# Closing passages of a four-layer graph network: relation products taken head by head on four row tiles, and relation rows copied first on ScalarE

## What is computed

```python
k = _typed_linear(x, Wk, bk, node_type).reshape(n, H, DH)
q = _typed_linear(x, Wq, bq, node_type).reshape(n, H, DH)
v = _typed_linear(x, Wv, bv, node_type).reshape(n, H, DH)
kt = jnp.einsum('nhd,rhde->rnhe', k, a_rel)
vt = jnp.einsum('nhd,rhde->rnhe', v, m_rel)
...
att = (q[dst] * k_e).sum(-1) * mu[edge_type] / np.sqrt(DH)
```

## Time and profile before

| | |
|---|---|
| median of 3 runs | 10143.94 us (10141.95 to 10145.79) |
| the profiled execution | 10142.34 us, its span 10140.3 us |
| PE busy | 2087.1 us (21%) |
| PEld busy | 1860.1 us (18%) |
| DVE busy | 5894.1 us (58%) |
| ACT busy | 3016.3 us (30%) |
| POOL busy | 6842.0 us (67%) |

### The profile page before, as it was taken

How to read it: one execution, slowest core, us unless ns; L and a number is a source line. 1 busy time by engine, 2 the same in 40 slices (tenths; PEclk the granted TensorE clock), 3 DMA queues, 4 the chain that set the end, 5 groups by cost and what they waited for, 6 DMA issues and landing times. The chain is left out here.

```text
span 10140.3 us, 57816 instructions
## 1 busy us (share of the span) xinstructions
PE 2087.1 (21%) x14986; PEld 1860.1 (18%) x14986; DVE 5894.1 (58%) x9620; ACT 3016.3 (30%) x3211; POOL 6842.0 (67%) x7186
## 2 busy tenths in 40 slices
PE   4555465551000000004500008100023000110002
PEld 3555465550000000003400006100012000110002
DVE  8777565553545555556588876688875322432225
ACT  6333233331223332232255442354531000110002
POOL 2777677777777777774377753677743777667773
PEclk9999955555555555556855559555555555555556
DMA  4511111112333333334466654566641333223331
GB/s 99 201 28 28 31 36 34 33 29 59 98 99 114 113 112 106 104 113 137 149 215 209 215 177 152 184 210 213 216 139 59 106 106 103 91 90 103 107 107 58
DMA packets 489971, 1161.75 MB, mean 115 GB/s; under 512 B 183257, under 2 KB 278828, under 8 KB 431532
## 3 DMA queue, kind: packets, MB, share of 16 engines
q0 software_dynamic: 255936, 474.70, 17.6%
q1 hardware_dynamic: 203756, 628.83, 16.5%
q10 hardware_dynamic: 29952, 54.54, 2.1%
HBM read 669.62 MB, written 487.92 MB: 114 GB/s over the span
## 5 line engine op out<-in xcount | busy, mean ns | idle before, releaser
L832 POOL DMA_INDIRECT slots<-REC,plc_idx x1664 | 1597.7, 960 | 554.7 <-issue 505.9
L1238 POOL DMA_INDIRECT l_swp_G<-table,KVI x1664 | 1573.3, 946 | 529.1 <-issue 506.3
L940 POOL DMA_INDIRECT l_G<-table,OTHI x1664 | 1583.3, 952 | 513.3 <-issue 506.2
L1490 POOL DMA_INDIRECT l2s_G<-table,OTHI x832 | 785.1, 944 | 428.6 <-issue 253.3
L1490 POOL DMA_INDIRECT l3s_G<-table,OTHI x832 | 786.4, 945 | 301.6 <-issue 253.2
L703 PEld LDWEIGHTS plc_pr<-plc_seen,plc_otf 128*128 128x128 f32 x3328 | 842.5, 323 | 21.3 <-issue 11.9
L703 PE MATMUL plc_pr<-plc_seen,plc_otf 128*128 128x49 f32 x3328 | 844.0, 408 | 11.1 <-DVE plc_seen L618 11.0
L1073 DVE TENSOR_TENSOR l_LB<-l_RE,l_G 128x64 f32<-128x64 f32 x104 | 29.4, 283 | 1026.5 <-DMA l_G<-table,OTHI 1026.3
L1340 DVE SCALAR_TENSOR_TENSOR l_swp_QS<-l_swp_QS,KEEP,l_swp_QX 128x128 f32<-128x128 f32 x1664 | 589.4, 354 | 36.9 <-DMA l_swp_QX<-queries 9.5
L1099 DVE TENSOR_TENSOR_SCAN l_X<-l_AW,l_X 128x2244 f32<-128x2244 f32 x104 | 502.5, 4832 | 3.6
L1399 DVE TENSOR_TENSOR_SCAN l_swp_X<-l_swp_AW,l_swp_X 128x2244 f32<-128x2244 f32 x104 | 501.5, 4822 | 0.1
(11 more groups left out here) (495 smaller groups left out, 9906.7 us busy)
## 6 DMA issues: line engine op xcount, KB each, us to landing
sums<-l_ROW SPq DMA_DIRECT2D x104, 1088.0 KB, 4.3
sums<-l_swp_ROW SPq DMA_DIRECT2D x104, 1088.0 KB
l_swp_QX<-queries SPq DMA_DIRECT2D x104, 1024.0 KB, 7.8
queries<-plc_zrow SPq DMA_DIRECT2D x33, 1664.0 KB
sums<-l3s_ROW SPq DMA_DIRECT2D x52, 1032.0 KB, 4.4
plc_low<-low_rows ACTq DMA_DIRECT2D x208, 256.0 KB, 3.3
sums<-l2s_ROW SPq DMA_DIRECT2D x52, 1024.0 KB, 4.4
table<-t_row SPq DMA_DIRECT2D x98, 512.0 KB, 2.6
```

The lines of the kernel that those rows point to most:

```text
L832: pool.indirect_dma_start(out=slots, out_offset=bass.IndirectOffsetOnAxis(ap=idx[:, c % IB, j:j + 1], axis=0), in_=g.REC[:, c * CH + j, :] ...
L940: pool.indirect_dma_start(out=G[:, c % GR, j, :], out_offset=None, in_=table, in_offset=bass.IndirectOffsetOnAxis(ap=g.OTHI[:, side(c), x: ...
L1238: pool.indirect_dma_start(out=G[:, c % GR, j, :], out_offset=None, in_=table, in_offset=bass.IndirectOffsetOnAxis(ap=index[:, c * CK + j:c ...
L1490: pool.indirect_dma_start(out=G[:, c % GR, j, :], out_offset=None, in_=table, in_offset=bass.IndirectOffsetOnAxis(ap=g.OTHI[:, k, c * CK + ...
```

## The change

The relation products are taken head by head: 8 matmuls a block (keys and values x 4 heads), each with 32 rows of `kv` and 32 rows of a dense `bd` as operands and 128 columns (4 relations x 32). Head `h` starts at partition 32h, and writes PSUM bank `h`: keys in columns 0 to 127, values in columns 128 to 255. All four banks belong to one block, so `relate(n)` now waits until block n-1 is copied, where it waited for block n-2. The zeros of `bd` go, and with them their memset and the wait for it; `mu` is laid out a word for each partition and relation, by four small loads in place of one. Both halves of a row are copied by ScalarE (`pack_rows`), as its first work in a step; VectorE copies neither.

```diff
-            bd = s.sb("bd", [P, 2, R, D])
-            mu = s.sb("mu", [P, R * H])
+            bd = s.sb("bd", [P, 2, R, HD])
+            mu = s.sb("mu", [P, R])
...
-                sp.dma_start(mu[:, :], a.mu[tables].rearrange("(o r) h -> o (r h)", o=1).to_broadcast([P, R * H])).then_inc(rel_ok, 16)
-                sp.wait_ge(cleared, 1)
+                with nc.allow_non_contiguous_dma(reason="a word for each head and relation, once"):
+                    for h in range(H):
+                        sp.dma_start(mu[h * HD:(h + 1) * HD, :],
+                                     a.mu[tables][:, h:h + 1].rearrange("r o -> o r").to_broadcast([HD, R])).then_inc(rel_ok, 16)
...
-                    sp.wait_ge(packed_k, n + 1)
-                    sp.wait_ge(packed_v, n + 1)
+                    sp.wait_ge(packed, n + 1)
...
-            if not gcn:
-                if closes_l0:
-                    v.memset(g.X[:, NB - 1, :], 0.0)
-                v.memset(bd[:, :, :, :], 0.0)
+            if closes_l0:
+                v.memset(g.X[:, NB - 1, :], 0.0)
...
-            def pack_keys(n):
-                b = n % 2
-                v.wait_ge(related, n + 1)
-                if n >= 2:
-                    v.wait_ge(stored[b], 16 * (n // 2))
-                v.tensor_copy(row[:, b, :, 0:D], pk[:, 2 * b, :].rearrange("p (r w) -> p r w", r=R)).then_inc(packed_k, 1)
...
                 if n >= 2:
-                    act.wait_ge(related, n - 1)
+                    act.wait_ge(related, 2 * H * (n - 1))
...
-            def pack_values(n):
+            def pack_rows(n):
                 b = n % 2
-                act.wait_ge(related, n + 1)
+                act.wait_ge(related, 2 * H * (n + 1))
                 if n >= 2:
                     act.wait_ge(stored[b], 16 * (n // 2))
-                act.activation(row[:, b, :, D:2 * D], pk[:, 2 * b + 1, :].rearrange("p (r w) -> p r w", r=R),
-                               ACT.Copy).then_inc(packed_v, 1)
+                for m in (0, 1):
+                    o = act.activation(row[:, b, :, m * D:(m + 1) * D].rearrange("p r (h e) -> p r h e", h=H),
+                                       pk[:, :, m * P:(m + 1) * P].rearrange("p h (r e) -> p r h e", r=R), ACT.Copy)
+                o.then_inc(packed, 1)
...
                 if not gcn:
+                    if 0 <= s_ - 2 < NB:
+                        pack_rows(s_ - 2)
                     if 0 <= s_ < NB:
                         keep_kvq(s_)
-                    if 0 <= s_ - 2 < NB:
-                        pack_values(s_ - 2)
...
                 pe.wait_ge(kv_kept, n + 1)
-                if n >= 2:
-                    pe.wait_ge(packed_k, n - 1)
-                    pe.wait_ge(packed_v, n - 1)
-                pe.matmul(pk[:, 2 * b, :], kv[:, b, 0, :], bd[:, 0, :, :].rearrange("p r d -> p (r d)"), start=True, stop=True)
-                pe.matmul(pk[:, 2 * b + 1, :], kv[:, b, 1, :], bd[:, 1, :, :].rearrange("p r d -> p (r d)"),
-                          start=True, stop=True).then_inc(related, 1)
+                if n >= 1:
+                    pe.wait_ge(packed, n)
+                for m in (0, 1):
+                    for h in range(H):
+                        own = slice(h * HD, (h + 1) * HD)
+                        o = pe.matmul(pk[:, h, m * P:(m + 1) * P], kv[own, b, m, :],
+                                      bd[own, m, :, :].rearrange("p r e -> p (r e)"), start=True, stop=True)
+                        o.then_inc(related, 1)
```

More of the change, by code:

```diff
@@ L1651, in turn_layer @@
             pk = s.ps("pk", [P, 4, 512])
-            turned_h, masked_h, made_kvq, kv_kept, q_kept, related, packed_k, packed_v = (s.sem(x) for x in (
-                "turned_h", "masked_h", "made_kvq", "kv_kept", "q_kept", "related", "packed_k", "packed_v"))
+            turned_h, masked_h, made_kvq, kv_kept, q_kept, related, packed = (s.sem(x) for x in (
+                "turned_h", "masked_h", "made_kvq", "kv_kept", "q_kept", "related", "packed"))
             put = [s.sem(f"put{r}") for r in range(4)]
@@ L1736, in _ @@
                     sp.dma_start(w3[:, m, :, :], Wm[tables].rearrange("t i o -> i t o")).then_inc(rel_ok, 16)
-                sp.dma_start(mu[:, :], a.mu[tables].rearrange("(o r) h -> o (r h)", o=1).to_broadcast([P, R * H])).then_inc(rel_ok, 16)
-                sp.wait_ge(cleared, 1)
+                with nc.allow_non_contiguous_dma(reason="a word for each head and relation, once"):
+                    for h in range(H):
+                        sp.dma_start(mu[h * HD:(h + 1) * HD, :],
+                                     a.mu[tables][:, h:h + 1].rearrange("r o -> o r").to_broadcast([HD, R])).then_inc(rel_ok, 16)
                 for m, rel in enumerate((a.a_rel, a.m_rel)):
                     for h in range(H):
-                        sp.dma_start(bd[h * HD:(h + 1) * HD, m, :, h * HD:(h + 1) * HD],
+                        sp.dma_start(bd[h * HD:(h + 1) * HD, m, :, :],
                                      rel[tables, :, h].rearrange("r d e -> d r e")).then_inc(rel_ok, 16)
@@ L1948, in _ @@
             if not gcn:
-                v.wait_ge(rel_ok, 16 * 12)
+                v.wait_ge(rel_ok, 16 * 15)
                 link(v.tensor_scalar(mu[:, :], mu[:, :], float(HD) ** -0.5, None, ALU.mult))
-                keys = bd[:, 0, :, :].rearrange("p r (h e) -> p (r h) e", h=H)
-                v.tensor_tensor(keys, keys, cols3(mu[:, :]).to_broadcast([P, R * H, HD]), ALU.mult).then_inc(scaled, 1)
+                v.tensor_tensor(bd[:, 0, :, :], bd[:, 0, :, :], cols3(mu[:, :]).to_broadcast([P, R, HD]), ALU.mult).then_inc(scaled, 1)
             for s_ in range(-3, NB + LAG):
@@ L1960, in _ @@
                         mask_h(s_ + 1)
-                    if 0 <= s_ - 2 < NB:
-                        pack_keys(s_ - 2)
                 else:
@@ L2134, in _ @@
                     if s_ == 0:
-                        pe.wait_ge(rel_ok, 16 * 12)
+                        pe.wait_ge(rel_ok, 16 * 15)
                         pe.wait_ge(scaled, 1)
```

## The result

The changed kernel takes 10061.84 us (median of 4 runs, 10059.76 to 10066.9); the kernel before, on the same chip, 10142.94 (4 runs, 10140.65 to 10145.79). The ratio is 0.992, with a 95% interval of 0.9907 to 0.9933: 81 us faster.

A forecast was written before the change was run, and what follows sets the result against it. TensorE was taken to bound both passages, its relation products setting the time for blocks 4 to 46. Savings of 22.5 us in t0 and 21.9 in t1, together 44.4 off 10142.3, gave 10098; range 10068 to 10178.

The forecast's parts named there:

- the sixteen records: A step's relation products on TensorE, two records for each of eight matmuls: 0.90 us taken, in place of 1.77.
- the three bounds: Possible cost of the relation products' records in a step: 1.79 us in a line, 0.90, or 0.45 with four heads side by side.
- the case in which neighbours in the stream wait: TensorE's relation products: a head's two records queue and the next head comes behind both, 0.90 us; chance 0.46.
- full overlap: Rival for TensorE's relation products: four heads side by side, 0.45 us, step 4.05, 81 us gained, 10061; chance 0.12.
- Changing the tiling: TensorE, twice in a step: idling when the array's tiling mode changes, 0.18 us each, 0.36 in all, bounds 0.22 and 0.46.
- Ordinary steps: Steps of t0 and t1 without part 6 of the norm: from 5.01 to 4.50 us, 3.24 of it unchanged.
- Part 6: Part of the norm in five steps of t0: ScalarE's root comes 0.48 us earlier, step from 5.99 to 5.51 us.
- The start: Ahead of the first scatters of queries: memset gone, loads earlier; nothing gained in t1, 0.7 us taken in t0.
- Copies, VectorE, end: ScalarE's two 603 ns copies fit the slack; VectorE loses 0.68 us a step, no bound; GpSimd's chain covers the end.
- The slower rival: Weight loads on TensorE share one path: products 2.15 us with tiling changes, step 5.39, +27.7 us, 10170; chance 0.30.

The follow-up runs named there:

- twice the set: Changed kernel with the eight relation products issued two times in every step, same outputs written again: 10094.27 us, steps of 4.49 to 4.50 us.
- one tile: Changed kernel with all eight relation products on the 32 rows of head 0: 10163.88 us, steps of 5.37 us.
- head-by-head order: Changed kernel with the two loops of the relation products exchanged, keys then values for each head: 10060.44 us, steps of 4.07 to 4.08 us.
- full rows: Changed kernel with relation matrices stretched with zeros to 128 rows for each head, so no row tiles: 10142.03 us, steps of 5.08 to 5.09 us.
- pairs: Changed kernel with the relation products of two blocks issued one after the other, in every second step: 10044.13 us, two steps 7.76 us.
- the copies alone: Kernel before with only the copies changed, both halves of a row copied by ScalarE ahead of `keep_kvq`: 10137.86 us, ratio 0.9996.
- (one, two, four): Row tiles holding the relation products; four is the changed kernel, two puts heads 2 and 3 on the rows of heads 0 and 1: 10113.61 us.
- eight buffers: Changed kernel with eight buffers for queries and eight semaphores `put` in place of four: 10039.74 us.
- the norm earlier: Changed kernel with the parts of the closing norm in t0 run one step earlier on VectorE and ScalarE: 10058.3 us.

## Why the prediction was right or wrong

**The step that failed** is the price of the sixteen records, 0.90 us in the sum: "if one head's second record runs beside the next head's first, a head costs one record: 8 x 0.112 = 0.90 us", and the reason for it, "the next head comes behind both". They cost 0.44 us (twice the set), four rounds of 0.11. Two records on the same rows do stand in a line, as I said (one tile: 5.37 us a step). But the next head does not stand behind them: by the head-by-head order, not even four records of a tile hold up the other tiles. The forecast was 36 us too high, and this term alone is 81 steps x 0.45 = 36. The lowest of the three bounds was the right one, and I had given it a chance of 0.12. I gave 0.46 to the case in which neighbours in the stream wait, without a row that showed one tile waiting for another.

That the time met *full overlap* to 1 us is in part luck. That rival's sum for the two passages is 81 us; they gained 79.0, and 3.3 us lie outside them.

The Trainium skill ("TensorE: Matmul & The Clock Gate", section on packing small matmuls) led to 0.58, between the measured 0.44 and my 0.90, and nearer than what I chose. Its factor of 3.07 is for 512 columns; here, with 128, sixteen records went from 16 x 0.110 = 1.76 us on one tile to 0.44 on four, a factor of 4.0.

**Changing the tiling**: 0.36 taken, 0.29 (full rows against one tile) to 0.34 (pairs) measured. What is left of the step, 4.05 - 3.24 - 0.44 = 0.37, is a little more; full rows leave 5.08 - 3.24 - 1.79 = 0.05 too. The one-row bias matmul gave a fair size, though no run shows that it runs as a 32-row tile: 0.23 us of idling ahead of its load at half clock, 0.16 ahead of the first relation load at full clock, and the rest at the way back. What the Trainium skill ("TensorEngine Tiling (Array Packing)", Key Properties) says, that a change of tiling mode drains the engine, agrees with this pause of 0.16 us. Without overlap the change does lose, as the run on one tile shows.

**Ordinary steps**: the rest of a step, 3.24 us, stood still, and 43 steps of a passage were on the path. For t1 alone that gives 43 x (5.01 - 4.05) = 41.3. From the first scatter of queries to the last it measured 41.8 (222.94 before, 181.16 after). The whole passage gave 41.4, but two other things cancel in it: the gathers ahead of the first scatter took 1.6 us less (66.47, then 64.90), and the last scatter landed 2.3 us later.

**Part 6**: right. 5.51 is what the copies alone give. With row tiles it is 5.57; all three kernels with row tiles in each step (one, two, four) have 5.57 whatever the records cost, full rows 5.51. The 0.06 is what the transpose takes longer when it comes behind row tiles.

**The start**: wrong in sign in t0. I took 0.7 us gained; block 4's queries were copied 69.07 us after the passage's first gather, before 67.91. The scatter started 66.20 us after the first gather, before 64.17, behind gathers that took 2 us longer (in t1 they took 1.6 less), and ScalarE's copy, now without slack, waited for it; behind the wait TensorE had about 3 us at half clock. I had also written that TensorE has no longer pauses than before: with shorter steps it comes to the scatter sooner and waits longer, 3.28 us in t0 where it did not wait, 10.83 in t1 where it was 6.77. In t1 the release stayed on the scatter's landing, as said.

**Copies, VectorE, end**: 597 ns a copy, no wait for `packed` but two at the ends, no step behind the start held up by VectorE but those with part 6. As predicted. The end still hangs on GpSimd's chain, as said, but its wait for the last scatter became 2.3 us longer in t1 and 0.5 in t0, which I had not foreseen.

**The slower rival**, weight loads in a line, is the one-tile kernel: its mechanism is real for one tile, and its price was right (5.39 said, 5.37 measured). What decides is that each row tile has its own line. Whether four banks are needed for that was not tried.

## What to carry to other kernels

Block-diagonal weights padded with zeros hold all 128 rows of the array: 5.08 us a step here, and 4.05 for the same products on four row tiles. On row tiles they cost the longest line of one tile, in both orders tried, plus 0.3 us for going into row tiles and back: so put as many tile products together as PSUM holds, as the pairs did. And once a step gets shorter, look at the buffers that hid a late transfer: four query buffers covered 20 us of steps before and 16 after, and taking the wait out was worth at least as much as halving the changes of tiling. Most of that wait had stood in t1 all along: its step across block 4 took 14.59 us before the change, in place of 5.01.

## What the runs showed that I had not expected

- Order among row tiles is nearly free: 0.02 us a step between two and four records of a tile in succession.
- A weight load's price does not depend on its rows either: 0.110 us for 32, 0.112 for 128.
- After 3.28 us of idling the clock fell not in the pause but about 1.5 us into the work behind it (1.00, then 0.50); after 10.83 us it was at 0.50 from the first matmul on.
- The last scatter of t1 and the transfer behind it stand 5.4 to 6.0 us apart in the four kernels with steps of 4.05 to 4.08 us (the changed one, head by head, eight buffers, the norm earlier), and at most 3.8 in all the others. The cause is open.
